# One kernel, four layers on one core: the first period of the mix phase in another order on VectorE, and both routing steps with another order of sending and placing

## What is computed

```
x = x + attention(norm(x))     # linear attention with 8 heads, rotary positions, a 3-tap convolution
x = x + experts(norm(x))       # 8 experts, the best 2 of each token
x = x + mix(norm(x))           # RWKV: time mix, then channel mix
x = x + experts(norm(x))       # the same experts again

# experts
scores = softmax(x @ gate_w.T); top_scores, sel = top_k(scores, 2)
order = argsort(sel_flat, stable=True)          # tokens sorted by expert
y = (silu(x_sorted @ w1[e]) * (x_sorted @ w3[e])) @ w2[e]
out = zeros.at[tok_sorted].add(y * scores_sorted)

# channel mix, the second half of the mix layer; lx2 is xn2 one token earlier
fk = (xn2 * mk + lx2 * (1 - mk)) @ f_w_key      # 256 to 1024
fr = (xn2 * mr + lx2 * (1 - mr)) @ f_w_recept
x = x + sigmoid(fr) * (square(relu(fk)) @ f_w_value)
```

## Time and profile before

| | |
|---|---|
| runs | 1417.42 us median of 3 (1417.21 to 1418.65) |
| the profiled execution | 1421.28 us, its span 1419.6 us |
| mean granted clock of TensorE | 0.967 of 2.4 GHz |
| busy over the span | PE 94%, DVE 64%, ACT 48%, POOL 45% |
| longest chain at the end | DMA out_x<-second_y,second_add_token 20% of the span |

### The profile page before, as it was taken

One profiled execution on the slowest core, in us unless ns is written; L12 is line 12 of the kernel. 1 busy time (PEld: TensorE's weight loads), 2 busy tenths in 40 slices (PEclk: granted clock), 3 DMA queues, 4 the chain that ended last, 5 costly groups with the idle time before them and its releaser, 6 DMA issues. The chain is left out here.

```text
span 1419.6 us, 27938 instructions
## 1 busy us (share of the span) xinstructions
PE 1339.8 (94%) x7618; PEld 1130.6 (80%) x7619; DVE 904.4 (64%) x2174; ACT 684.1 (48%) x1543; POOL 631.9 (45%) x583
## 2 busy tenths in 40 slices
PE   6999997899999999976899999998989999999997
PEld 4999986788888888833677787777868888888886
DVE  5777889544444444458888898888774544444453
ACT  4577756233333333355587679766643333333332
POOL 4768663345555555423232223222213555555553
PEclk9899997899999999998899999999989999999999
DMA  8575854566665333370000000000317666633332
GB/s 275 190 270 200 291 224 135 168 160 168 161 159 112 60 56 57 46 226 0 1 15 31 0 30 30 30 1 31 120 61 215 162 159 168 161 71 56 57 53 41
DMA packets 100873, 157.84 MB, mean 111 GB/s; under 512 B 10256, under 2 KB 60688, under 8 KB 100816
## 3 DMA queue, kind: packets, MB, share of 16 engines
q1 hardware_dynamic: 73120, 118.67, 24.6%
q0 software_dynamic: 27264, 37.82, 16.5%
q10 hardware_dynamic: 432, 0.66, 0.2%
HBM read 95.89 MB, written 61.21 MB: 111 GB/s over the span
## 5 line engine op out<-in xcount | busy, mean ns | idle before, releaser
L1402 POOL DMA_INDIRECT out_x<-second_y,second_add_token x71 | 112.7, 1587 | 154.0 <-DMA out_x<-second_y,second_add_token 128.6
L1402 POOL DMA_INDIRECT x_rows<-first_y,first_add_token x70 | 111.3, 1590 | 148.8 <-DMA x_rows<-first_y,first_add_token 105.9
L1393 POOL DMA_INDIRECT xs<-normed_rows,gather_token x140 | 138.8, 991 | 44.2 <-issue 40.0
L1497 DVE TENSOR_TENSOR first_hT_lo<-bank,first_hT_hi 128x512 fp32r<-128x512 f32 x71 | 49.1, 691 | 160.1 <-ACT first_hT_hi L1430 160.1
L1497 DVE TENSOR_TENSOR second_hT_lo<-bank,second_hT_hi 128x512 fp32r<-128x512 f32 x71 | 49.1, 692 | 159.8 <-ACT second_hT_hi L1430 159.8
L166 PE MATMUL bank<-ring,first_xT_hi 128*128 (+1 forms) x284 | 119.1, 419 | 0.1
L166 PE MATMUL bank<-ring,second_xT_hi 128*128 (+1 forms) x284 | 118.7, 418 | 0.1
L168 PE MATMUL bank<-ring,first_xT_lo 128*128 (+1 forms) x284 | 112.7, 397 | 0.0
L167 PE MATMUL bank<-ring,first_xT_hi 128*128 (+1 forms) x284 | 112.7, 397 | 0.0
L168 PE MATMUL bank<-ring,second_xT_lo 128*128 (+1 forms) x284 | 112.5, 396 | 0.0
L167 PE MATMUL bank<-ring,second_xT_hi 128*128 (+1 forms) x284 | 112.4, 396 | 0.0
(11 more groups left out here) (458 smaller groups left out, 3912.3 us busy)
## 6 DMA issues: line engine op xcount, KB each, us to landing
ring<-split_weights SPq DMA_DIRECT2D x192, 256.0 KB, 3.0
a_wraw<-in_L_ffn_w SPq DMA_DIRECT2D x21, 512.0 KB, 6.4
split_weights<-a_whi SPq DMA_DIRECT2D x21, 512.0 KB, 2.6
split_weights<-a_wlo SPq DMA_DIRECT2D x21, 512.0 KB, 3.5
normed_rows<-xg SPq DMA_DIRECT2D x16, 528.0 KB, 3.2
x_rows<-x SPq DMA_DIRECT2D x8, 512.0 KB, 7.0
x<-x_rows SPq DMA_DIRECT2D x8, 512.0 KB, 5.8
out_x<-x SPq DMA_DIRECT2D x8, 512.0 KB, 3.2
```

The lines of the kernel that those rows point to most:

```text
L1393: nc.gpsimd.indirect_dma_start(xs[q][:], None, normed_dram[:], bass.IndirectOffsetOnAxis(ap=gather_token[q][:], axis=0)).then_inc(loaded[q ...
L1402: nc.gpsimd.indirect_dma_start(x_dram[:], bass.IndirectOffsetOnAxis(ap=add_token[q][:], axis=0), y[q], None, compute_op=ALU.add).then_inc( ...
L1497: nc.vector.tensor_tensor(hT_lo[par][:].rearrange("p k t -> p (k t)"), th_bank[par][:], hT_hi[par][:].rearrange("p k t -> p (k t)").bitcas ...
```

## The change

Three places are edited. In the mix phase's period 0, DVE does begin(2) directly behind time_output(0), and mix_channel(0) is written out as first_mix_channel, with low_weights(0) behind the mix of xfk and low_weights(1) behind that of xfr. In both routings, late_places, late_hots, late_totals and final_places of the last late tiles become one function, last_places, in which the steps that give places and those that give the totals take turns, the block hots stand behind the base, and the row hots behind that; the copy of the lanes to lanef falls away there. send_tokens raises its semaphore once for each of the four tiles and no longer once for a group, and place_tokens goes tile by tile. After attention, ACT sends groups 1 to 4 one place earlier in its row. The wide products ahead of the last placings are 4 and no longer 6 after attention, and 9 and no longer 12 after mix.

```diff
@@ OwnSteps @@
-    def link(self, ins, passed=None):
-
+    def mark(self, ins):
         self.k += 1
         ins.then_inc(self.sem, 1)
+
+    def settle(self):
         self.engine.wait_ge(self.sem, self.base + self.k)
+
+    def link(self, ins, passed=None):
+
+        self.mark(ins)
+        self.settle()
...
@@ hot_blocks @@
     if n >= depth:
-        dve.wait_ge(r.sent_ready, n - depth + 1)
+        dve.wait_ge(r.sent_ready, CH * (n - depth + 1))
@@ send_tokens @@
     for j in range(CH):
         t = n * CH + j
-        last = nc.scalar.activation(r.sent[n % depth][:, :, j, :], r.block_hot[n % len(r.block_hot)][:, :, j, :], ACT.Copy,
-                                    scale=const.token[:, t:t + 1])
-    last.then_inc(r.sent_ready, 1)
+        nc.scalar.activation(r.sent[n % depth][:, :, j, :], r.block_hot[n % len(r.block_hot)][:, :, j, :], ACT.Copy,
+                             scale=const.token[:, t:t + 1]).then_inc(r.sent_ready, 1)
@@ final_places becomes last_places @@
+def last_places(nc, dve, own, r, const, lane, n):
+
+
+    dve.wait_ge(r.count_done, 2 + n)
...
+    own.link(nc.vector.tensor_tensor_scan(cells[:, 1:EX * tiles], r.all_late[n][:, 0:EX * tiles - 1], keep[:, 1:EX * tiles], 0.0,
+                                          ALU.add, ALU.mult))
+    nc.vector.tensor_tensor(rank, earlier, r.before_late[n].rearrange("p (e t) -> p e t", t=tiles), ALU.add)
+    own.link(nc.vector.tensor_tensor(r.total, r.total, r.earlier_late[n][:, :, tiles - 1], ALU.add))
+    nc.vector.tensor_tensor(rank, rank, r.offset.unsqueeze(2).to_broadcast([P, EX, tiles]), ALU.add)
+    own.link(nc.vector.tensor_tensor(r.total, r.total, r.all_late[n][:, tiles - 1:EX * tiles:tiles], ALU.add))
+    nc.vector.tensor_tensor(chosen, r.hot[:, :, :, lo:hi], rank.unsqueeze(1).to_broadcast([P, TOPK, EX, tiles]), ALU.mult)
     own.link(nc.vector.tensor_scalar(r.counti, r.total, float(P - 1), None, ALU.add))
+    nc.vector.tensor_reduce(r.posf[:, :, part], chosen.rearrange("p k e t -> p k t e"), AXX, ALU.add)
...
     own.link(nc.vector.tensor_tensor_scan(end[:], const.ones[:, 0:EX].bitcast(F32), r.used, 0.0, ALU.mult, ALU.add))
-    own.link(nc.vector.tensor_tensor(base[:], end[:], r.used, ALU.subtract))
-    own.link(nc.vector.tensor_tensor(r.moved, base[:], r.base, ALU.subtract))
+    own.mark(nc.vector.tensor_tensor(base[:], end[:], r.used, ALU.subtract))
+    for g in groups:
+        hot_blocks(nc, dve, r, lane, g)
+    own.settle()
+    own.mark(nc.vector.tensor_tensor(r.moved, base[:], r.base, ALU.subtract))
+    for g in groups:
+        hot_rows(nc, dve, r, lane, g)
+    own.settle()
@@ place_tokens @@
-    pe.wait_ge(r.sent_ready, n + 1)
-    for k in range(TOPK):
-        for j in range(CH):
+    for j in range(CH):
+        pe.wait_ge(r.sent_ready, CH * n + j + 1)
+        for k in range(TOPK):
@@ attention, ACT behind the last period @@
             route_before(B)
+            send_tokens(nc, act, route, const, 1)
             gate_rows(B)
-            send_tokens(nc, act, route, const, 1)
+            send_tokens(nc, act, route, const, 2)
             gate_logits(B)
-            send_tokens(nc, act, route, const, 2)
+            send_tokens(nc, act, route, const, 3)
             row_exp(B)
-            send_tokens(nc, act, route, const, 3)
+            send_tokens(nc, act, route, const, 4)
             row_finish(B)
-            send_tokens(nc, act, route, const, 4)
             send_tokens(nc, act, route, const, 5)
@@ attention, PE @@
-            wait_warm(6)
+            wait_warm(4)
@@ mix, DVE, new @@
+            def first_mix_channel():
+                dve.wait_ge(t_emptied, round_xn2(0) + 1)
+                m2.round(0)
+                m2.link(nc.vector.tensor_tensor(dT[:], xn2T[:, :, 1:N + 1], xn2T[:, :, 0:N], ALU.subtract))
+                mixed(xn2T, ((xfk, "f_time_mix_k"),), 0, mix2_ready, 0)
+                low_weights(0)
+                mixed(xn2T, ((xfr, "f_time_mix_r"),), 0, mix2_ready, 1)
+                low_weights(1)
@@ mix, DVE, period @@
                 if static(b, 0):
+                    dve.wait_ge(x_in[2], 16 * (B - 2))
+                    begin(b + 2)
                     mixed(xnT, ((xr, "time_mix_r"),), 1, mix_ready, 2)
                 if has_next(b, 1):
                     exponents(b + 1)
-                if static(b, 0):
-                    low_weights(0)
...
-                mix_channel(b)
                 if static(b, 0):
-                    low_weights(1)
-                    dve.wait_ge(x_in[2], 16 * (B - 2))
-                    begin(b + 2)
+                    first_mix_channel()
+                else:
+                    mix_channel(b)
                 low_key(b)
@@ mix, PE @@
-            keep_busy(nc, xb_[4][:], fk_hi[:, 0, 0:P], fk_hi[:, 0, 0:N], 12)
+            keep_busy(nc, xb_[4][:], fk_hi[:, 0, 0:P], fk_hi[:, 0, 0:N], 9)
```

More of the change, by code:

```diff
@@ L443, in late_totals @@
         own.link(nc.vector.scalar_tensor_tensor(out=r.offset, in0=r.base, scalar=float(P), in1=r.total, op0=ALU.mult, op1=ALU.add))
-def final_places(nc, own, r, const):
-    end, base = r.placed.end, r.placed.base
+def last_places(nc, dve, own, r, const, lane, n):
+    dve.wait_ge(r.count_done, 2 + n)
+    lo, hi = r.late[n]
+    tiles, part = hi - lo, slice(lo, hi)
+    groups = range(lo // CH, hi // CH)
+    keep = const.keep_late if tiles == TL else const.keep_last
+    earlier, rank, chosen = r.earlier_late[n], r.rank_late[n], r.chosen_late[n]
+    end, base = r.placed.end, r.placed.base
+    cells = earlier.rearrange("p e t -> p (e t)")
+    own.link(nc.vector.tensor_tensor_scan(cells[:, 1:EX * tiles], r.all_late[n][:, 0:EX * tiles - 1], keep[:, 1:EX * tiles], 0.0,
[5 more added lines that the diff above has]
+    nc.vector.tensor_tensor(chosen, r.hot[:, :, :, lo:hi], rank.unsqueeze(1).to_broadcast([P, TOPK, EX, tiles]), ALU.mult)
@@ L450, in final_places @@
     own.link(nc.vector.tensor_scalar(r.counti, r.total, float(P - 1), None, ALU.add))
+    nc.vector.tensor_reduce(r.posf[:, :, part], chosen.rearrange("p k e t -> p k t e"), AXX, ALU.add)
     own.link(nc.vector.tensor_scalar(r.counti, r.counti, 7, None, ALU.arith_shift_right))
+    nc.vector.tensor_copy(r.posi[:, :, part], r.posf[:, :, part])
     own.link(nc.vector.tensor_scalar(r.used, r.counti, 1.0, None, ALU.max))
+    nc.vector.tensor_scalar(r.block_at[:, :, part], r.posi[:, :, part], 7, None, ALU.arith_shift_right)
@@ L453, in final_places @@
+    nc.vector.tensor_scalar(r.lane_at[:, :, part], r.posi[:, :, part], P - 1, None, ALU.bitwise_and)
     own.link(nc.vector.tensor_tensor_scan(end[:], const.ones[:, 0:EX].bitcast(F32), r.used, 0.0, ALU.mult, ALU.add))
-    own.link(nc.vector.tensor_tensor(base[:], end[:], r.used, ALU.subtract))
-    own.link(nc.vector.tensor_tensor(r.moved, base[:], r.base, ALU.subtract))
+    own.mark(nc.vector.tensor_tensor(base[:], end[:], r.used, ALU.subtract))
+    for g in groups:
+        hot_blocks(nc, dve, r, lane, g)
@@ L1168, in _ @@
             softmax_end(B)
[L1169 to L1172, removed]
+            last_places(nc, dve, placing, route, const, lane, 0)
             block_tables(nc, placing, blocks, placed, const)
@@ L2090, in mix_channel, with low_weights @@
                 mixes(m2, xn2T, ((xfk, "f_time_mix_k"), (xfr, "f_time_mix_r")), b, mix2_ready)
+            def first_mix_channel():
[6 more added lines that the diff above has]
+                low_weights(1)
+            def low_weights(h):
+                part = slice(h * F // 2, (h + 1) * F // 2)
+                dve.wait_ge(fk_hi_ready, 1)
+                nc.vector.tensor_tensor(fk_lo[:, :, part], fk_raw[:, :, part], fk_hi[:, :, part].bitcast(F32),
+                                        ALU.subtract).then_inc(fk_lo_ready, 1)
             def low_key(b):
@@ L2219, in _ @@
             first_quotient()
[L2221 to L2225, removed]
             def period(b):
@@ L2303, in _ @@
             softmax_end(B - 1)
[L2304 to L2307, removed]
+            last_places(nc, dve, placing, route, const, const.lane, 1)
             row_tokens(nc, dve, placing, route, const)
```

## The result

The changed kernel takes 1410.37 us (median of 4 runs, 1409.68 to 1410.85), the kernel before 1418.04 beside it: ratio 0.9938 [0.9926, 0.9951], 7.7 us less. The forecast was 1410.9 us, 6.5 us less than 1417.42. Its profiled execution took 1410.74 us for a span of 1409.0, that of before 1421.28 for 1419.6. PE is busy for 95% of the span and no longer 94.

A forecast was written before the change was run, and what follows sets the result against it. PE was taken to be stalled in mix's first period by DVE's order, through POOL and ACT. 6.9 + 0.65 - 1.0 = 6.5 us off 1417.4 gave 1410.9 us, range 1407.3 to 1413.6.

The forecast's parts named there:

- part 1: Mix period 0: begin(2) moved ahead of xr and low_weights(0) behind xfk end PE's 5.65 us wait; gain about 6.9 us.
- the upper bound: Mix period 0: if POOL is quick beside begin(2), PE's product becomes the limit and the gain is 7.4 us.
- the 0.6 us at period 1's key products: Mix period 1: PE waits 0.6 us for ACT's high key copy, at 719.2 against 718.6, leaving 6.9 us gained.
- xr 1.85 us later costs nothing: Mix period 0: begin(2) delays xr, but PE's receptance product ends at 666.2, ahead of transposes at 666.7; cost nothing.
- a limit of 0.5 us on top of 6.9: Mix period 0: with POOL quick, PE's product becomes the limit and 0.5 us is added, 7.4 us in all.
- Part 2: Routing after attention: earlier sends and two fewer warm-up products, less losses at the lower clock; gain about 0.65 us.
- Part 3: Routing after mix: nine warm-up products leave the last group cold, at the lower clock; loss about 1.0 us.
- cold, the group ends later: Routing after mix: placed at the lower clock, the last group ends at 1056.35 and not 1055.7, 0.65 us lost.
- everything warm, POOL quick: Rival: both routings at the higher clock and POOL quick gain 9.5 us, giving 1407.9 us; chance 0.2.
- DVE did not become the bound: Rival: DVE becomes the bound of mix periods 0 and 1, leaving 4.6 us gained, 1412.8 us; chance 0.2.
- the stall did not stay: Rival: hidden(0) still waits behind norm(2) in mix period 0, only routing parts left, -0.35 us, 1417.8 us; chance 0.05.
- DVE did not wait for x: Rival: in mix period 0, begin(2) makes DVE wait at 659.4 for loads of x; change slower, chance 0.03.

The follow-up runs named there:

- experiment 3: Kernel before with only ACT's row changed: in mix period 0, norm(2) goes behind the fourth hidden group; 1412.75 us against 1418.7, ratio 0.9955.
- 4: Kernel before with only begin(2) moved directly behind time_output(0), both low_weights where they were; 1410.16 us against 1418.61, ratio 0.9944.
- experiment 5: Changed kernel with DVE's mix of xr ahead of begin(2); median 1408.21 us against 1410.28 for the changed kernel.
- experiment 6: Changed kernel with wide products back at 6 and 12: 1409.77 us; the same with the mix of xr ahead of begin(2): 1407.17 us.
- experiment 2: Kernel before with both routing edits alone, mix period 0 as it was; 1417.11 us against 1418.7, ratio 0.9988.
- experiment 9: Changed kernel with ACT's sends of groups 1 to 4 at their old places after attention; 1410.35 us in one execution.

## Why the forecast held, and where it did not

The mechanism of part 1 was right: experiment 3 removes the same stall from ACT's side, 4 shows that begin(2) alone carries it. It gave 7.4 us and not 6.9, at the upper bound. Two terms were off. I had POOL's operations of period 0 as slow beside bn_stats as beside the scans; the power took 1.04 us. The Trainium skill (GPSIMD Engine Reference, Key points) names two inputs from SBUF as a case of contention with VectorE, which the scans have and bn_stats does not. The trace agrees: 1.04 beside the statistics, 1.84 beside the scans. And the 0.6 us at period 1's key products did not come: they start at 715.04 and not at 725.95, 10.9 us earlier like all of period 1, and PE did not wait for them. DVE's second addition of time_output(1), which I had 6.5 us earlier, came 10.9 earlier, 7.4 if measured from T, and only waited for PE there:

```profile
697.35 0.69 DVE L2214 TENSOR_TENSOR b_xb<-b_xb,bank 128x512 f32<-128x512 f32 x1 [0.25 <-PE bank L2355]
```

One step of part 1 was wrong though its sum came out: that xr 1.85 us later costs nothing. The cover that I named were the transposes at 666.7, and they waited for POOL's scales, which the same edit made quick. With that wait shortened PE's product behind xr was the last to end, and the delay was PE's. The forecast had this as a limit of 0.5 us on top of 6.9; experiment 5 puts the price at 2.4 to 2.6 us from T to xn(2), of which 1.8 is the first transposes' (9.65 us behind T against 11.47) and the rest the clock; in experiment 6 it was 3.5.

That the sum still fits is in part luck. From the low products to xn(2) the stage gave 7.6 us (15.07 to 7.49), my 5.7 for the wait and 1.8 for the clock. Ahead of that stand two terms that I had at nothing: the first transposes came 1.0 us sooner behind T (12.46 to 11.47), POOL's gain less xr's delay, and the key products up to the low ones took 1.1 us more (5.15 to 6.25), since more of them ran at the lower clock. The two cancel.

Part 2 gave 1.09 us for 0.65, at the lower clock as forecast (0.7 to 1.5 over the five profiles with these edits; the profile of experiment 2, at 1.5, had group 7 partly warm). The end of group 5 came 10.53 us behind the gate products, for 12.64 before: 2.1 gained for my 1.75. The sends' share is 0.75 (experiment 9), the other 1.4 came without them, and with them go the waits of 0.22 and 0.92 us ahead of groups 2 and 3. Placing by tiles is the edit that lets PE begin a group before its last tile is sent, but no run has it alone.

Part 3 failed in the profile of the changed kernel: +0.36 us for -1.0. The step that failed is "cold, the group ends later"; DVE's row was as I had it (block hots 2.27 us behind the scan for my 2.3). In the changed kernel the clock was at 0.50 from about 1039.5 on and rose before the nine products ended, which took 3.87 us; it stayed at 1.00 through PE's idle time and the group. In the kernel of experiment 2 it was at 0.50 from 1046 to 1054, and the nine took 4.19. All three profiles with group 7 warm have the nine at 3.8 to 3.9 us, the three with it cold at 4.19: the group is warm where the clock rises within the nine. What makes it do so is open. But over all profiles with nine products group 7 took 1.05 us in three and 1.86 in three, and the stage 11.4 in the one case and 12.6 to 12.8 in the other, against 11.78 before: a gain of 0.4 or a loss of 0.8 to 1.0, where I had one of the two. With twelve it was never over 1.24 us in eight profiles.

What the sum lacked: the value product of period 7, -1.0 us, no edit near it. The edited stages gave 8.8 us for a forecast of 6.5, and this loss brought the total back towards it, so the forecast was closer than its terms. That is luck too.

The rival "everything warm, POOL quick" had the POOL half right, and the second routing in half of the profiles; its own sum is 1407.9, where the last lines of the prediction say 1407.3. DVE did not become the bound (period 1 begins 10.90 us earlier, like the transposes before it), the stall did not stay, and DVE did not wait for x.

## What to carry to other kernels

When an engine waits at a copy whose engine is idle, look at what stands ahead of the copy in that engine's row, and at the chain behind that instruction; moving either end of it works. A step moved forward delays what it passes, and the cover for that must be priced after the edit, since the edit may shorten the very chain that gave the cover. For parts of 1 to 2 us, cut two profiles at landmarks and compare stages: medians of five runs did not tell such parts apart here, and one profile didn't tell a clock's level that comes out either way.

## What the hardware showed that I had not expected

- POOL's small operations beside DVE: the first two of rstd took 0.23 us each beside bn_stats, 0.52 and 0.60 beside xr; in the kernel before 0.53 beside xr and 1.67 while DVE went from xr to the scans. The power took 1.04 beside the statistics and 1.84 beside the scans and rho. The price depends on which DVE instruction runs, not only on whether one does.
- The clock in untouched work: the same 32 products in period 7 took 7.74 to 8.83 us behind an idle time of 5.3 us, in twelve profiles, and 7.07 in both with wide products in it.
- The two clock effects went together. With nine wide products, the three profiles with group 7 warm had a value product of 8.71 to 8.78 us in period 7, and the three with it cold 7.96 to 8.25. In period 7 the clock fell 3.7 us after PE stopped in the changed kernel's profile and 1.6 us after in that of the kernel before, and the later fall went with the later rise. What sets the moment is not shown; nothing was tried on it.
- In the first routing, six wide products brought the clock up ahead of group 6 in all four profiles of the old order (0.96 to 0.98 us a group) and in none of three of the new one (1.71), where they start 2 us sooner behind the gate products. The number of products alone does not decide it.
